# A chain of gated blocks on one core: expert-slot norms moved by half a feed-forward, a rounding pass moved to ScalarE, and the last products of a quantised block moved behind the next attention's first scores

## The reference

```python
x = x + tanh(g_ffn[1])   * L1_ffn(layernorm(x))        # gated dense feed-forward, 256 -> 1024 -> 256
x = x + tanh(g_xattn[2]) * L2_xattn(ctx, layernorm(x)) # 0.6*sigmoid(si + sj + b) + 0.4*layernorm(x)
x = x + tanh(g_ffn[2])   * L2_ffn(layernorm(x))        # the quantised block, below
x = x + tanh(g_xattn[3]) * L3_xattn(layernorm(x), ctx) # attention, 16 heads of 16, 4 key groups
x = x + tanh(g_ffn[3])   * L3_ffn(layernorm(x))        # soft mixture: 16 experts x 128 slots

def bitlinear158(x, w, b):     # used twice in L2_ffn
    xq = act_quant(rms_norm(x))     # per row: round(x * 127/max|x|), clipped, and scaled back
    return xq @ weight_quant(w).T + b   # weights -1, 0, 1 times a mean
# L2_ffn: layer_norm(gelu(silu(bitlinear158(x, w1, b1)))) -> bitlinear158(., w2, b2)
# L3_ffn: logits = l2norm(layernorm(x)) . l2norm(mu, over its 256 rows), mu is 256 x (16*128)
```

## Time and profile before

| | us |
|---|---|
| median of 3 runs (lowest, highest) | 1324.08 (1322.42, 1325.32) |
| the profiled execution | 1326.74 |
| span of its trace | 1325.0 |
| TensorE busy | 1057.4 |
| VectorE busy | 740.0 |
| ScalarE busy | 525.4 |
| GpSimd busy | 328.2 |
| down products of the first half of L1_ffn begin | 838.27 |
| down products of the second half begin | 895.98 |
| last addition of the quantised half 0 ends | 952.28 |
| last addition of the quantised half 1 ends | 1025.07 |
| soft mixture's first logits | 1107.6 |

### The profile page before, as it was taken

How to read it: one execution, slowest core, us unless ns; L and a number is a source line. 1 busy time by engine, 2 the same in 40 slices (tenths; PEclk the granted TensorE clock), 3 DMA queues, 4 the chain that set the end, 5 groups by cost and what they waited for, 6 DMA issues and landing times.

```text
span 1325.0 us, 19053 instructions
## 1 busy us (share of the span) xinstructions
PE 1057.4 (80%) x6622; PEld 672.3 (51%) x6625; DVE 740.0 (56%) x1684; ACT 525.4 (40%) x883; POOL 328.2 (25%) x626
## 2 busy tenths in 40 slices
PE   4245999999999678778798889984252888899997
PEld 2124888888888533233355645533232443475565
DVE  3654444544454646685655512457777765676644
ACT  1111333233333457465444540133344654445543
POOL 5103334433443445433333220001030400000000
PEclk9999999999999768898799998988665898999999
DMA  6000111111230300000000020002000000000000
GB/s 150 9 0 19 43 48 47 40 44 48 50 103 7 135 2 2 2 2 2 2 2 2 4 112 0 0 0 48 1 2 0 3 2 1 1 1 9 8 9 8
DMA packets 62441, 32.06 MB, mean 24 GB/s; under 512 B 47104, under 2 KB 61072, under 8 KB 62112
## 3 DMA queue, kind: packets, MB, share of 16 engines
q1 hardware_dynamic: 62368, 31.10, 8.8%
HBM read 29.64 MB, written 1.05 MB: 23 GB/s over the span
## 4 chain that ended last, share of the span: by engine, by line
PE 69%; DVE 20%; ACT 4%; issue 4%; POOL 1%; SPq 0%; DMA 0%; POOLq 0%; DVEq 0%; ACTq 0%; PEldq 0%
PE bank L692 15%; PE bank L708 7%; PE bank L800 4%; PE bank L1084 3%; DVE mx L2120 3%; PE bank L915 2%; PE bank L883 2%; PE bank L1016 2%; PE bank L1270 2%; PE bank L845 2%; PE bank L1253 2%; PE bank L1064 2%; PE bank L1255 2%; PE bank L1117 2%; PE bank L1100 1%
## 5 line engine op out<-in xcount | busy, mean ns | idle before, releaser
L2120 DVE TENSOR_REDUCE mx<-bank 128x2 f32<-128x512 f32 (+1 forms) x176 | 118.1, 689 | 88.6 <-PE bank L1016 44.8
L1594 ACT ACTIVATE prob<-bank 128x512 f32<-128x512 f32 x176 | 102.7, 597 | 100.1 <-PE bank L1064 78.3
L1433 ACT ACTIVATE hhi<-hh 128x512 fp32r<-128x512 f32 x72 | 45.5, 632 | 153.1 <-DVE hh L1957 140.5
L1953 DVE TENSOR_TENSOR hu<-bank,sg 128x512 f32<-128x512 f32 x64 | 44.3, 692 | 101.6 <-PE bank L692 101.6
L692 PE MATMUL bank<-xh,wh 128*128 128x512 f32 x288 | 91.5, 398 | 0.7 <-POOL wl L2539 0.7
L692 PE MATMUL bank<-xh,wl 128*128 128x512 f32 x288 | 90.5, 395 | 0.0
L692 PE MATMUL bank<-xlo,wh 128*128 128x512 f32 x288 | 90.1, 394 | 0.0
L1945 DVE TENSOR_TENSOR hlo<-hh,hhi 128x512 fp32r<-128x512 f32 x72 | 57.1, 793 | 50.6 <-ACT hhi L1433 50.6
L2539 POOL TENSOR_TENSOR wl<-wraw,wh 128x512 fp32r<-128x512 f32 x72 | 80.4, 1117 | 13.0 <-POOL wh L2536 13.0
L1472 ACT ACTIVATE sg<-bank 128x512 f32<-128x512 f32 x72 | 43.1, 598 | 64.8 <-PE bank L692 64.8
L692 PEld LDWEIGHTS bank<-xh,wh 128*128 128x128 f32 x288 | 54.4, 189 | 14.6 <-POOL wl L2539 1.6
(11 more groups left out here) (456 smaller groups left out, 2321.5 us busy)
## 6 DMA issues: line engine op xcount, KB each, us to landing
wraw<-in_L_ffn_wg_dram SPq DMA_DIRECT2D x64, 64.0 KB, 2.3
wraw<-in_L_ffn_wu_dram SPq DMA_DIRECT2D x64, 64.0 KB, 2.4
wraw<-in_L_ffn_wd_dram SPq DMA_DIRECT2D x32, 128.0 KB, 2.5
l_raw<-in_L_ffn_w_dram SPq DMA_DIRECT2D x2, 1024.0 KB, 6.9
mun<-in_L_ffn_mu_dram SPq DMA_DIRECT2D x1, 2048.0 KB, 7.8
xs<-in_x_dram SPq DMA_DIRECT2D x1, 1024.0 KB, 5.9
w1s<-in_L_ffn_W_dram SPq DMA_DIRECT2D x2, 512.0 KB, 7.9
stage<-in_L_ffn_W_in_base_dram SPq DMA_DIRECT2D x1, 1024.0 KB, 7.0
```

Source lines behind the costliest of these rows:

```text
L1433: return act.activation(dst, src, ACT.Copy, scale=scale)
L1594: act.activation(t.prob[k][:, :], bank[3 + n % 2][:, :], ACT.Exp).then_inc(S("probs"), 1)
L1953: tt(hu[k % 2][:, :], bank[4 + (n + 1) % 4][:, :], sg[k % 2][:, :], ALU.mult).then_inc(once("up_used"), 1)
L2120: V.reduce_max(out_, bank[n % 3][:, :].rearrange("p (h t) -> p h t", h=heads), AX, negate=True)\
```

## The change

Three parts.

1. Slot norms: products, turning, spreading and scaling move from the first half of L1_ffn to the second, all four spreads now share bank 7, and two of them stand between down products. On VectorE `slot_norms` comes after `hidden(1, 4)`.
2. Rounding: VectorE's four passes of `l2_round_hidden` become ScalarE's, one directly before each quantising pass, in both halves. VectorE only signals that the scales are there.
3. Last products of half 1: `l2_round_hidden`, `l2_add`, the squares, rounding and `l2_last(1)` move from turn -1, k = 7 to turn 0, k = 7. `l2_shift(1)` stays in turn -1. The late products use banks 0 to 2 instead of 3 to 5 and wait for 24 maxima; `by_key(0, 0)` waits for the last `l2_pre`, `by_query` of group 3 for the last addition. `norm` of batch 2 moves from turn 0 to turn 1.

```diff
+L2_LATE_BANKS = ((4, 5, 6), (0, 1, 2))
-            b = L2_BANKS[h][n % 3]
+            b = (L2_BANKS if n < Q2T_USE[0] else L2_LATE_BANKS)[h][n % 3]
# TensorE
+                    if stream == "C" and n == 24:
+                        pe.wait_ge(S("l2_rows"), 2 * T0)
                     if stream == "C" and n == 0:
-                        pe.wait_ge(S("l2_rows"), 2 * T0)
+                        pe.wait_ge(S("l2_pre"), 16)
-                            if (sl, k) == (-1, 7):
+                            if (sl, k) == (0, 7):
                                 l2_last(1)
             for f in range(F1 // P):
                 gate_and_up(0, f)
-                if f == 1:
-                    slot_products()
-                if f == 3:
-                    turn_slot_parts()
...
             for f in range(1, F1 // P):
                 gate_and_up(1, f)
+                if f == 1:
+                    slot_products()
                 if f == 4:
                     turn_inputs(0)
                 if f == 5:
+                    turn_slot_parts()
                     l2_up(0, 0)
                     l2_up(0, 1)
                 if f == 6:
+                    spread_slots(0)
...
+            spread_slots(1)
             for i in range(T0):
                 down(1, i)
+                if i < 2:
+                    spread_slots(2 + i)
             l2_last(0)
# ScalarE
-                        if stream == "C" and k == 0 and inside(sl + 4) and groups[sl + 4][1] >= 2 and groups[sl + 4][2] == 0:
-                            if groups[sl + 4][1] == 2:
-                                act.wait_ge(S("ln_x"), 2)
-                            norm(groups[sl + 4][1])
+                        if stream == "C" and (sl, k) in ((1, 0), (2, 0)):
+                            act.wait_ge(S("ln_x"), 2)
+                            norm(sl + 1)
+            def l2_round_hidden(h, i):
+                act.wait_ge(S("l2_r2"), h + 1)
+                act.activation(h2[:, i, :], h2[:, i, :], ACT.Identity, bias=l2v[:, 57:58], scale=l2v[:, 52 + i:53 + i])\
+                    .then_inc(S("l2_r3"), 1)
             def l2_second_quantised(h, i):
-                act.wait_ge(S("l2_r2"), T0 * h + i + 1)
+                act.wait_ge(S("l2_r3"), T0 * h + i + 1)
-                            if (sl, k) == (-1, 7):
+                            if (sl, k) == (0, 7):
                                 for i in range(T0):
                                     l2_square(1, i)
                                 for i in range(T0):
+                                    l2_round_hidden(1, i)
                                     l2_second_quantised(1, i)
# VectorE
                                 l2_norm2(1)
                                 l2_shift(1)
+                            if (sl, k) == (0, 7):
                                 l2_round_hidden(1)
                                 l2_add(1)
                                 stats_of(step, 0.25, range(T0, 2 * T0))
...
-                for i in tiles:
-                    ts(h2[:, i, :], h2[:, i, :], l2v[:, 52 + i:53 + i], ROUND, ALU.mult, ALU.add).then_inc(S("l2_r2"), 1)
+                dve.sem_inc(S("l2_r2"), 1)
```

More of the change, by code:

```diff
@@ L1279, in slot_products @@
                     for cc in range(DC):
-                        last = mm(bank[6][:, e:e + 1], mu2[:, cc, e * SS:(e + 1) * SS], ones[:, 0:1], start=cc == 0, stop=cc == 1)
+                        last = mm(bank[7][:, e:e + 1], mu2[:, cc, e * SS:(e + 1) * SS], ones[:, 0:1], start=cc == 0, stop=cc == 1)
                 last.then_inc(S("mu_products"), 1)
@@ L1291, in spread_slots @@
                     pe.wait_ge(S("mu_partsT"), 1)
-                if ch >= 2:
-                    pe.wait_ge(S("mu_normed"), ch - 1)
+                else:
+                    pe.wait_ge(S("mu_normed"), ch)
                 for e in range(4 * ch, 4 * ch + 4):
-                    last = mm(bank[6 + ch % 2][:, e % 4 * SS:(e % 4 + 1) * SS], sel[:, e, :], cmT[:, :], start=True, stop=True)
+                    last = mm(bank[7][:, e % 4 * SS:(e % 4 + 1) * SS], sel[:, e, :], cmT[:, :], start=True, stop=True)
                 last.then_inc(S("mu_spread"), 1)
             def l2_free(h, n):
-                if n >= 3:
+                if h == 1 and Q2T_USE[0] <= n < Q2T_USE[0] + 3:
+                    pe.wait_ge(S("maxed"), 24)
+                elif n >= 3:
                     name, count = L2_FREED[n - 3]
@@ L1304, in l2_free @@
                     pe.wait_ge(S("ffn_out"), T0)
-                    pe.wait_ge(S("mu_normed"), 4)
+                    pe.wait_ge(S("cT2"), 2)
                 elif n == 0:
@@ L1751, in _ @@
                 gate_silu(0, f)
-                if f == 4:
-                    act.wait_ge(S("mu_partsT_ps"), 1)
-                    copy(cmT[:, :], bankb[7][0:96, 0:P]).then_inc(S("mu_partsT"), 1)
             gate_silu(1, 0)
@@ L1764, in _ @@
             gate_silu(1, 5)
+            act.wait_ge(S("mu_partsT_ps"), 1)
+            copy(cmT[:, :], bankb[7][0:96, 0:P]).then_inc(S("mu_partsT"), 1)
             l2_silu(0, 0)
@@ L1776, in _ @@
             for i in range(T0):
+                l2_round_hidden(0, i)
                 l2_second_quantised(0, i)
@@ L2250, in _ @@
                    for i in range(2 * T0)])
-            step(ts(l2v[:, 0:8], l2v[:, 0:8], l2b[:, 0:1], None, ALU.add), V.memset(l2v[:, 56:57], -ROUND),
+            step(ts(l2v[:, 0:8], l2v[:, 0:8], l2b[:, 0:1], None, ALU.add), V.memset(l2v[:, 56:57], -ROUND), V.memset(l2v[:, 57:58], ROUND),
                  ts(rowsD["L2_ffn_b2"][:, :], rowsD["L2_ffn_b2"][:, :], gates[:, 6:7], None, ALU.mult))
@@ L2276, in slot_norms @@
                 dve.wait_ge(S("mu_products"), 1)
-                step(V.tensor_copy(cmx[:, :], bank[6][:, 0:SE]))
+                step(V.tensor_copy(cmx[:, :], bank[7][:, 0:SE]))
                 rsqrt(step, rbc[:, 0:SE], cmx[:, :])
@@ L2417, in _ @@
             hidden(1, 4)
+            slot_norms()
             l2_pre(0, 0)
@@ L2423, in _ @@
             hidden(1, 6)
+            scale_slots(0)
             hidden(1, 7)
+            scale_slots(1)
             l2_stats(0, 0)
@@ L2427, in _ @@
             add_down(1, 0)
+            scale_slots(2)
             l2_stats(0, 2)
@@ L2430, in _ @@
             add_down(1, 1)
+            scale_slots(3)
             l2_norm2(0)
```

16 lines of the change are left out of this document (2 added, 14 removed), and 1 row of the table STAGES.

## The result

The changed kernel takes 1339.3 us (median of 4 runs, 1336.5 to 1342.5) against 1324.2 before; the ratio is 1.0101 with a 95% interval of [1.0072, 1.0131]. By the ratio it is slower by some 13 us, by the medians by 15.1; the forecast was 1334.7, range 1325 to 1340. Its profiled execution took 1336.46, 2.8 less than its median, where the one before lay 2.5 above, so the spans of the two traces differ by less than the medians.

What follows compares the result with a forecast made beforehand. TensorE paces the dense feed-forward, then VectorE's statistics, scaling and reduction lead a serial chain. Terms -13.7, +6.5, +1.2, +3.0 give -3.0 up to the reduction, +13.6 to turn 2: +10.6 on 1324.08, 1334.7 us; range 1325 to 1340.

Steps and rivals of the forecast that it cites:

- A: The forecast: the last products' chain grows more than the scores it lets pass; +10.6 us, range 1330 to 1338, chance 0.70.
- Slot products in the second half +6.5, bounds to +8.9: L1_ffn's second half: products and slow step cost 12.1, TensorE's wait and slow step there save 5.6; bounds +4.5 to +8.9.
- Small norm steps +1.2: Second half of L1_ffn: VectorE's small instructions, spreads and scalings of the slot norms cost +1.2, bounds +0.5 to +1.7.
- Rounding in half 0, +3.0: First quantised half: four dependent ScalarE round-and-quantise pairs take 9.2 to 9.3 us; cost +3.0, bounds +2.0 to +4.2.
- Z 3.0 us earlier: Z, the end of VectorE's large reduction in the second quantised half (1008.85 before), comes 3.0 us earlier.
- Z to the last addition 32.5: From VectorE's large reduction: exponentials, squares, small steps, ScalarE passes and last products take 32.5 us, where it was 16.2.
- To the turning of group 2's maxima 11.3: Turn 1: TensorE waits for maxima GpSimd splits after queries and keys, 11.3 us after the last addition.
- To turn 2, 7.0: From turning group 2's maxima to turn 2's first score by keys: 6.3 us before, 7.0 partly at the low clock.
- Behind turn 2, nothing: Turns after turn 2: operations are made turn by turn from the same group, so nearly all should shift along.
- B: Turn 1: the wait for maxima behind the new normalisation does not hold; total +0.7, about 1325; chance 0.08.
- D: Turns 3 to 8: idle TensorE time takes up the delay, making the kernel faster, 1321.9; chance 0.10.
- C: TensorE's clock stays up: -1.9 after the large reduction, -2.0 behind slot products, -0.7 in turn 1; 1330; chance 0.12.

Runs made afterwards that it cites:

- run 1: Kernel before with only the slot norms moved, rounding left on VectorE and last products in turn -1; 1321.8 us, ratio 0.9963.
- run 9: Changed kernel with 42, 20 and 40 matmuls nobody reads filling three TensorE waits around the last products and in turn 1; 1329.6 us, ratio 1.0033.
- run 4: Kernel before with only the last products of half 1 one turn later; 1336.4 us, ratio 1.0081.
- run 6: Changed kernel with GpSimd splitting the maxima of group 2 at the head of turn 0's queries; 1330.6 us, ratio 1.0039.
- run 11: Changed kernel with rounding on VectorE, squares ahead of the fifth exponential and group 2's maxima ahead of the queries; 1319.4 us, ratio 0.9955.
- run 8: Kernel before with slot norms moved, plus batch 2's VectorE statistics and ScalarE normalisation later in turn 0; 1315.5 us, ratio 0.9915.

## Why the prediction was right

The time, 1339.3, lies above A's own range, 1330 to 1338, and 0.7 under the upper end of the one stated, so the range held with little to spare; as a change, +13.4, it is within A's +6 to +14. Part by part:

- *First half -13.7:* measured -13.73.
- *Slot products in the second half +6.5, bounds to +8.9:* 64.84 against 57.71 us, +7.1, in the profiled execution, and 1.6 more in the second one. The products took 10.32 and the slow step behind them 1.9 more; the wait of 3.16 went, as said. Both lie within the bound.
- *Small norm steps +1.2:* +0.6 (by the end of the down products, 6.0 us earlier than before).
- *Rounding in half 0, +3.0:* +2.8 between the traces, +3.15 between run 1 and the changed kernel, each up to the last addition of half 0. Four pairs took 9.36 (9.2 to 9.3 forecast). The estimate by the Trainium skill ("ScalarE: Activation LUTs", section What ACT_TABLE_LOAD costs), 2.27 a tile, is 0.04 to 0.06 under the 2.31 to 2.33 of the rows.
- *Z 3.0 us earlier:* 3.4.
- *Z to the last addition 32.5:* 32.56. The parts were less exact: 7.2 for 6.8 to the eighth exponential, 4.2 for 4.8 for the squares, 3.4 for 3.4, 9.35 for 9.4, 8.4 for 8.1. The squares' 1.19 of the earlier trace rows was VectorE's pace: each had waited for a shifted tile. Alone, they start 1.04 apart.
- *To the turning of group 2's maxima 11.3:* 11.32.
- *To turn 2, 7.0:* this step was mis-sized, 8.54. I gave 0.7 for the clock; run 9, at a granted clock of 1.00, took 2.5 less.
- *Behind turn 2, nothing:* 2.2, not in the sum at all. I let everything shift along and did not ask at which clock. 1.3 of it lies between turns 3 and 5, at a granted clock of 0.81 instead of 0.90; the rest was not traced. It is gone in run 9 and, with no wait filled, in runs 4, 6 and 11, so it is not the price of the late part's waits.
- *The rivals.* B fell: TensorE waited 9.03 us for GpSimd; taking that order away gives 3.9. D fell: run 4, with nothing but the late place, pays 10.7. C did not happen, the clock was 0.55 to 0.76, but it was worth more than I gave it: the scores laid between the waits did not hold the clock; filling the waits wholly does. In run 9 that gave 2.5 in turn 1, where C had 0.7, and 1.8 over the last products, where C had nothing; C's other places, the half turn after Z and the step behind the slot products, were not filled.

The sign and the path were right; the total of the terms, +10.6, is 3 us short. From the first gate-and-up step on the changed kernel's trace is 13.9 longer: 0.4 less than forecast up to Z, 1.5 more to turn 2, 2.2 more behind it. The term to turn 2 is the clock, as run 9 shows. The one behind turn 2 goes with a lower clock for 1.3 of its 2.2, but why the clock fell there stays open. What I can't account for is the rest between trace totals and ratios: runs 8 and 11 are 7.2 and 1.7 us shorter than before from the first gate-and-up step on, and 11.3 and 6.0 by their ratios. The start of that step varies by 6 us between the traces; run 11's is the latest, 784.21, in the slowest of its executions (1326.86, median 1319.4). Half of it is there in the first 160 us, in code that no edit touches: the same table load of ScalarE starts at 159.62 in the kernel before, at 159.66 in run 11 and at 156.58 in run 8. What varies there was not tried.

## What to carry to other kernels

Before work is moved behind other work on an in-order engine, list what waits for it in every queue: here ScalarE's squares stood behind its exponentials, GpSimd's maxima behind its queries and keys, and in the order before ScalarE's second exponential behind the normalisation, none of which had to do with them. Moving them gave 3.4, 3.9 and 2.1 us in b. Price what stands behind a new TensorE wait at the low clock, not at the duration of the profile. And try the parts of a change one by one: one of these three gains 5 us, and the others hid it. The edits also changed the time of a stage that none of them touches, by up to 2.3 us between turns 3 and 5, with the granted clock: read a gain in the stretch that was edited, and apart from it what lies behind.

## What the runs showed of the hardware

- VectorE's rounding pass over 128x1024 (multiply and add, f32) is 0.75 us long, and four in a row take 2.74; ScalarE's same pass is 1.24 long.
- A ScalarE pass that needs the result of the one before it on its own engine starts 0.04 us after that ends (925.18 + 1.24 to 926.46); independent ones overlap by about 0.1.
- A wait of TensorE costs twice: run 9 filled 22.5 us of three waits with work for nobody (9.24, 4.48 and 8.80; the second is not among the rows shown), and the stretch that holds them became 4.3 us shorter. The whole kernel became some 8 us faster than the changed one, but 2.85 of this lie behind turn 2, where runs without filling gained as much.
